# A post-norm attention and mixture-of-experts kernel: other places in the attention schedule, the tail of the last two batches moved, weight splits regrouped

## What is computed

```
qkv = x @ c_attn_w.T + c_attn_b                  # 16 heads of 16
q_lat, k_lat, v_lat = q@q2l.T+b, k@kv2l.T+b, v@kv2l.T+b     # 32 wide
q_lat, k_lat = rope(q_lat), rope(k_lat)
att = softmax(causal((q_lat @ wqk.T + b) @ k_lat.T * 32**-0.5))
x  = layernorm(x + (att @ v_lat @ l2o.T + b) @ cproj.T + b)
gates = top 2 of 8 of softmax(x @ gate_w)
y = sum over the two experts: w2 . gelu(ln(w1 . x + b1)) + b2, weighted
out = layernorm(x + ln(y + x))
```

## Time and profile before

| | us |
|---|---|
| median of 3 runs | 2278.8 |
| the three runs | 2265.12, 2283.3, 2278.8 |
| the profiled execution | 2262.56 |
| its span, first to last instruction | 2260.8 |
| granted TensorE clock, mean share of full speed | 0.949 |

### The profile page before, as it was taken

The page is one execution under the profiler, slowest core; times in us unless marked ns, Lnnn a source line. Parts: engine busy times, 40 slices in busy tenths (PEclk is TensorE's granted clock), DMA queues, the critical chain, the costliest instruction groups (busy, mean ns, idle before and its releaser), DMA issues. The chain is left out here.

```text
span 2260.8 us, 43557 instructions
## 1 busy us (share of the span) xinstructions
PE 2031.2 (90%) x12109; PEld 1414.5 (63%) x12109; DVE 1683.3 (74%) x4941; ACT 1403.8 (62%) x3324; POOL 1428.6 (63%) x1696
## 2 busy tenths in 40 slices
PE   4799999999999999999999999995399999999785
PEld 3555655655655655655565565543299999999664
DVE  3677677677777778768767777735588888888598
ACT  1266657656656665666665665664188888888565
POOL 2364565676665685477567566544677777777575
PEclk7799999999999999999999999986699999999998
DMA  6565556556645555555555564425022222222593
GB/s 180 137 139 149 123 121 170 123 117 149 152 106 131 152 129 136 154 122 125 145 124 120 139 157 106 106 56 212 20 73 76 74 75 74 77 74 74 192 313 131
DMA packets 165759, 284.56 MB, mean 126 GB/s; under 512 B 54000, under 2 KB 78216, under 8 KB 165384
## 3 DMA queue, kind: packets, MB, share of 16 engines
q1 hardware_dynamic: 146264, 244.87, 42.7%
q0 software_dynamic: 17152, 35.87, 5.2%
q10 hardware_dynamic: 2112, 1.05, 0.2%
HBM read 100.11 MB, written 38.22 MB: 61 GB/s over the span
## 5 line engine op out<-in xcount | busy, mean ns | idle before, releaser
L603 ACT ACTIVATE probs<-scores_T 128x512 f32<-128x512 f32 (+3 forms) x1536 | 660.0, 494 | 286.2 <-PE scores_T L474 269.9
L881 POOL TENSOR_SCALAR_AFFINE_SELECT probs<-probs 128x256 f32<-128x256 f32 x512 | 211.6, 421 | 506.8 <-ACT probs L603 505.0
L774 DVE TENSOR_REDUCE neg_part<-ring 128x1 f32<-128x512 f32 x512 | 333.5, 686 | 166.4 <-PE ring L533 164.4
L533 PE MATMUL ring<-k_stack,q_stack_b 96*128 96x512 f32 (+3 forms) x1024 | 401.1, 416 | 28.9 <-DVE neg_max L779 26.7
L474 PE MATMUL scores_T<-q_stack_b,k_stack 98*128 98x512 f32 (+3 forms) x1024 | 358.2, 394 | 14.2 <-ACT probs L603 12.9
L491 PE MATMUL o_ps<-probs,v_ones 128*17 128x512 f32 (+3 forms) x3072 | 334.9, 509 | 17.4 <-POOL probs L881 17.4
L779 DVE CUSTOM_DVE_ANT_0 ring<-ring,mask 128x384 f32<-128x384 f32 (+3 forms) x512 | 241.7, 510 | 94.5 <-PE ring L533 89.5
L533 PEld LDWEIGHTS ring<-k_stack,q_stack_b 96*128 96x128 f32 x1024 | 197.0, 194 | 169.0 <-DVE neg_max L779 67.2
L779 DVE CUSTOM_DVE_ANT_0 ring<-ring,mask,neg_part 128x384 f32<-128x384 f32 (+3 forms) x512 | 258.8, 554 | 34.8 <-PE ring L533 32.5
L474 PEld LDWEIGHTS scores_T<-q_stack_b,k_stack 98*128 98x128 f32 x1024 | 193.2, 195 | 127.2 <-ACT probs L603 100.4
L1216 ACT ACTIVATE o_sb<-ht_ps,ln_b,ln_g 128x128 f32<-128x128 f32 x544 | 217.1, 448 | 76.2 <-PE ht_ps L1165 73.2
(11 more groups left out here) (207 smaller groups left out, 4624.3 us busy)
## 6 DMA issues: line engine op xcount, KB each, us to landing
u_rot<-u SPq DMA_DIRECT2D x128, 256.0 KB
k_stack<-u_rot SPq DMA_DIRECT2D x128, 256.0 KB
lat_w<-lat_split SPq DMA_DIRECT2D x32, 512.0 KB
q_stack_a<-u_rot SPq DMA_DIRECT2D x64, 256.0 KB
q_stack_b<-u_rot SPq DMA_DIRECT2D x64, 256.0 KB
k_stack<-u SPq DMA_DIRECT2D x64, 256.0 KB
y<-y_rows SPq DMA_DIRECT2D x32, 512.0 KB, 6.0
x_raw<-in_xT SPq DMA_DIRECT2D x16, 512.0 KB, 5.8
```

Source lines behind the costliest of these rows:

```text
L533: nc.tensor.matmul(out[:, 0:k1 - k0], q_stack[qb // 4][0:3 * L, row_buf(n, qb // 4), h, P * (qb % 4):P * (qb % 4) + P], k_stack[0:3 * L, n ...
L603: nc.scalar.activation(probs[:, s % 2, h, cols], sc[t % 3][:, HALF - w:HALF], ACT.Exp).then_inc(exp_done, 1)
L774: nc.vector.tensor_reduce(neg_part[:, n % 2, part_col], src[:], AX_X, ALU.max, negate=True).then_inc(max_taken, 1)
L881: nc.gpsimd.affine_select(both, both, [[0, 2], [1, P]], ALU.is_ge, zero, base=0, channel_multiplier=-1).then_inc(kept, 1)
```

## The change

Three things, all of order:

1. `PLACES` and `LAGS` get other numbers. Sorted, SyncE's order of DMAs stays the same but for one item (STORE of batch 6 comes before PACK of unit 29). On GpSimd, in g0, the first k-rope instruction now stands before a SCAT, the first Y behind the first add of the rope (before it until now), and the second Y behind the second add; in g1 a SCAT that stood behind the k-rope's second instruction (the first sine) stands behind its fourth (the first add); ZB and NORM move a few places. On VectorE the second X pair moves behind two S, the second KL behind one or two S, and the C items come at half a slot apart and not a whole one. On TensorE C moves likewise, the second U of k and the first WQ move behind one to three other items, and the four V come without other items between them. On ScalarE NX, KH's second half and E move.
2. For batch 6, NX, ZT and G get a pace of 3 slots (4 before), and STORE, R, E, CNT and SCAT come 8.125 slots earlier, SCAT at a pace of 1. ZB of batch 7 gets a pace of 1. The items of `LAST_TAIL` no longer get the `LAGS`, so NORM of batch 7 comes behind the last mask of unit 31, and not before the last two.
3. In the second block ScalarE splits eight weights before NX of the second half (four before); VectorE does W 0 to 3 between the two routing groups and 4 to 14 at the end (0 to 12 at the end before); GpSimd does W 15 alone (13, 14 and 15 before).

```diff
--- before.py
+++ after.py
@@ -176,25 +176,26 @@
 
 
 PLACES = {
-    "B": (-6, 0.25), "LAT": (-54.625, 0.125), "Uq": (-50.125, 1), "SWAPq": (-50.75, 0.125), "ROPEq": (-44.25, 0),
-    "WQ": (-41.5, 1.875), "QL": (-40.75, 1.75), "STACKq": (-34.375, 0.125), "Uk": (-43.625, 0), "SWAPk": (-39, 0.5),
-    "ROPEk": (-37.75, 0.5), "KH": (-35.75, 2.25), "KL": (-33.375, 2.125), "STACKk": (-30, 5.75),
-    "S": (-27.75, 22.375), "MT": (-2.375, 0), "MD": (-3.375, 0), "PV": (5.5, 2), "OE": (11.5, 16.125),
-    "PACK": (23.75, 0.25), "RCP": (28.625, 0.125), "INV": (22.25, 0), "Y": (35.375, 1), "X": (-60.375, 3.75),
-    "V": (-22.25, 0.5), "RES": (17.5, 0.5), "ZB": (30.375, 3), "C": (39.625, 1), "NORM": (52.375, 0),
-    "NX": (51.875, 4), "ZT": (56.75, 4), "G": (60, 4), "STORE": (85.5, 0), "R": (88.875, 0.375),
-    "CNT": (94.375, 0.25), "SCAT": (102.625, 3.625), "SPREAD": (34.375, 0), "E": (94.25, 0)}
+    "B": (-13.125, 0.25), "LAT": (-54.125, 0), "Uq": (-50.375, 1), "SWAPq": (-50.625, 0.625), "ROPEq": (-44.25, 0),
+    "WQ": (-41, 1.5), "QL": (-40.375, 1.75), "STACKq": (-32.75, 0), "Uk": (-43.5, 0.5), "SWAPk": (-39.5, 0.5),
+    "ROPEk": (-38.5, 0.5), "KH": (-35.375, 2.75), "KL": (-33.625, 3.125), "STACKk": (-30.375, 4.875),
+    "S": (-27.75, 22.375), "MT": (-2.375, 1), "MD": (-4.625, 0.75), "PV": (5.5, 2), "OE": (11.375, 16.125),
+    "PACK": (28.625, 0.5), "RCP": (28.625, 0), "INV": (22.875, 0.5), "Y": (35.75, 1.5), "X": (-61, 5),
+    "V": (-21.625, 0), "RES": (16.5, 2.125), "ZB": (30.5, 3.625), "C": (40, 0.5), "NORM": (51.75, 0),
+    "NX": (47.5, 4.375), "ZT": (56.875, 4), "G": (60.25, 4), "STORE": (79.75, 0.5), "R": (88.875, 0.375),
+    "CNT": (94.625, 1), "SCAT": (102.125, 3.625), "SPREAD": (37, 1.25), "E": (91.5, 0.375)}
 
 LAST_TAIL = {
     "PACK": (12, 16), "SUM": (13.5, 0), "INVERT": (14, 0), "EXPAND": (15.5, 0), "COPY": (16, 0), "Y": (17.5, 0),
     "C": (22, 0.5), "NORM": (24.5, 0)}
-
-
-LAGS = {"sync": {"INV": 5.625, "X": 1.25, "LAT": 0.875, "RES": 1.625, "STORE": -0.125, "STACK": -0.125, "SPREAD": 0.75, "SWAP": 0.125},
+LAST_UNIT = ("PACK", "SUM", "INVERT", "EXPAND", "COPY", "Y")
+
+
+LAGS = {"sync": {"INV": 9, "X": 2.375, "LAT": 0.875, "RES": 2.75, "STORE": 3.75, "STACK": 1, "SPREAD": -3.125, "PACK": -1, "MD": 0.375},
         "tensor": {},
-        "scalar": {"KH": 1, "E": -0.5, "OE": -0.25, "ZT": 0.375, "U": -0.25, "B": -0.125},
-        "vector": {"X": 1, "RCP": 0.75, "KL": -0.375, "S": -0.125, "G": -0.25, "C": -0.125, "NX": -0.5, "R": 0.375, "MT": -0.5},
-        "gpsimd": {"ZB": 1.25, "NORM": -2.625, "Y": 0.125, "SCAT": 1.75, "B": 0.25}}
+        "scalar": {"KH": 0.875, "E": 6.25, "OE": -0.125, "ZT": -0.625, "U": -0.25, "B": -0.375, "WQ": -0.5, "V": 0.125, "MT": -0.75, "NX": -0.125},
+        "vector": {"X": 1.5, "RCP": 0.625, "KL": -0.375, "S": -0.125, "G": -0.25, "C": -0.125, "NX": 5.75, "R": 0.5, "MT": -0.5, "QL": -0.75},
+        "gpsimd": {"ZB": -1.25, "NORM": -5.375, "Y": -0.625, "SCAT": 2.25, "B": 0.25, "ROPE": -0.25}}
 
 
 def attention_phase(nc, dram, wts, consts, xs, lat_dram, inv_dram, x1_dram, token_of_row, routes, tail, attention,
@@ -285,8 +286,15 @@
 
             def put(name, *items):
                 first, pace = LAST_TAIL[name] if n == UNITS - 1 and name in LAST_TAIL else PLACES[name]
-                if name == "SCAT" and b == B - 2:
-                    pace = 0.9
+                if b == B - 2 and name in ("NX", "ZT", "G"):
+                    pace = 3
+                    first = PLACES["ZT"][0] + 2.25 if name == "G" else first
+                if b == B - 2 and name in ("STORE", "R", "E", "CNT", "SCAT"):
+                    (zt, _), (gate, slow) = PLACES["ZT"], PLACES["G"]
+                    first -= gate + slow * (TB - 1) - (zt + 2.25 + 3 * (TB - 1))
+                    pace = min(pace, 1)
+                if b == B - 1 and name == "ZB":
+                    pace = 1
                 at.extend((first + pace * i, it) for i, it in enumerate(items))
 
             put("LAT", ("LAT", n))
@@ -344,7 +352,8 @@
         def order_of(engine):
 
             lag = LAGS[engine]
-            return [it for _, it in sorted(placed, key=lambda p: p[0] + lag.get(p[1][0], 0))]
+            own = lambda it: (it[0] in LAST_TAIL and it[1] == (UNITS if it[0] in LAST_UNIT else B) - 1)
+            return [it for _, it in sorted(placed, key=lambda p: p[0] + (0 if own(p[1]) else lag.get(p[1][0], 0)))]
 
         main = {engine: order_of(engine) for engine in LAGS}
         of_tiles = lambda name, *tbs: [(name, B - 1, tb) for tb in tbs]
@@ -974,14 +983,14 @@
         table_loads = [(limit, "limit"), (slot_no, "slot_no"), (tile_row, "tile_row"),
                        (base0, "base"), (rows2, "rows2")]
         weights = lambda a, b: [("W", w) for w in range(a, b)]
-        hi_order = (13, 0, 14, 15, 1, 2, 3, 4, 5, 6, 7, 8, 9, 10, 11, 12)
+        hi_order = (15, 0, 1, 2, 3, 4, 5, 6, 7, 8, 9, 10, 11, 12, 13, 14)
         upper = lambda a, b: [("W", w) for w in hi_order[a:b]]
         route = lambda v: [("R", v, i) for i in range(R_STEPS)]
-        late_act = (of_tiles("NX", 0, 1, 2, 3) + of_tiles("ZT", 0, 1, 2, 3) + upper(0, 4) + of_tiles("NX", 4, 5, 6, 7)
-                    + [("E", B - 1)] + of_tiles("ZT", 4, 5, 6, 7) + upper(4, 7) + [("E", B)] + upper(7, len(parts)))
+        late_act = (of_tiles("NX", 0, 1, 2, 3) + of_tiles("ZT", 0, 1, 2, 3) + upper(0, 8) + of_tiles("NX", 4, 5, 6, 7)
+                    + [("E", B - 1)] + of_tiles("ZT", 4, 5, 6, 7) + upper(8, 11) + [("E", B)] + upper(11, len(parts)))
         late_dve = (of_last("INVERT") + of_last("COPY") + of_tiles("G", 0, 1, 2, 3) + of_tiles("C", 4, 5, 6, 7) + route(B - 1)
-                    + of_tiles("G", 4, 5, 6, 7) + route(B))
-        late_pool = (of_last("Y") + [("W", 13), ("NORM", B - 1, 1)] + weights(14, len(parts))
+                    + weights(0, 4) + of_tiles("G", 4, 5, 6, 7) + route(B))
+        late_pool = (of_last("Y") + [("W", 15), ("NORM", B - 1, 1)]
                      + [("SCAT", B - 1, k, tb) for k in range(2) for tb in range(TB // 2)]
                      + [("SCAT", B, k, tb) for k in range(2) for tb in range(TB // 2, TB)])
 
@@ -1054,15 +1063,15 @@
                 then(nc.vector.tensor_scalar(expert_f[:], expert_f[:], float(E - 1), None, ALU.min))
                 nc.vector.tensor_copy(routes["expert"][:], expert_f[0:1, :]).then_inc(done, 1)
                 nc.vector.tensor_copy(routes["ones2"][:], rows2[:]).then_inc(done, 1)
-                vector_items(dve, weights(0, 13))
-                dve.wait_ge(w_lo_ready, 13)
+                vector_items(dve, weights(4, 15))
+                dve.wait_ge(w_lo_ready, 15)
                 dve.wait_ge(done, 3)
 
             @block.gpsimd
             def _(pool):
                 nc.gpsimd.memset(experts["b2"][:].bitcast(F32), 0.0).then_inc(b_zeroed, 1)
                 gpsimd_items(pool, late_pool, None)
-                pool.wait_ge(w_lo2_ready, len(parts) - 13)
+                pool.wait_ge(w_lo2_ready, len(parts) - 15)
                 pool.wait_ge(scattered, 16 * 2 * TILES)
 
     return experts
```

## The result

The changed kernel takes 2220.1 us (median of 4 runs, 2216.8 to 2222.6) against 2276.8 for the kernel before (median of 4 runs, 2265.1 to 2283.3): a ratio of 0.9756, 95% interval 0.9719 to 0.9792, so 2.4% or 56 us faster. The forecast was 24 us, and the range ended at 2235. The profiled executions lie 40.1 us apart (spans 2260.8 and 2220.7): the one before was among the fastest of its kernel, which the forecast carried over as a constant.

| | before | after | |
|---|---|---|---|
| start to unit 0 | 106.4 | 105.5 | -0.9 |
| the eight g0 units | 371.9 | 359.4 | -12.4 |
| the eight g1 units | 378.4 | 369.5 | -8.8 |
| the eight g2 units | 322.9 | 322.9 | -0.1 |
| the seven g3 units | 313.1 | 304.1 | -9.0 |

What follows compares the result with a forecast made beforehand. Attention, two thirds of the span, was taken as TensorE's, losing to idle time and a falling clock. Terms 6 + 7 + 8 - 3 + 4.4 + 2 = 24 us took 2278.8 to 2255; range 2235 to 2280.

Steps and rivals of the forecast that it cites:

- KL in g0: VectorE's KL in g0 is held less by GpSimd: 1.2 us in five units, 6 us (0 to 8).
- X in g1: First X pair in g1 starts during a scatter and is stretched less: 1.4 us in five units, 7 us.
- rival A: In g1 a scatter makes the cast wait as an add does, and the clock falls as before: 2270, chance 0.18.
- The clock: TensorE's clock falls less in five g1 units after shorter idle: about half of 15 us, 8 us (0 to 15).
- New waits: Eight C at half a slot can push S back: 0.5 us per batch in six batches, 3 us lost.
- rival C: In g0 VectorE becomes the bound under eight C and TensorE stands at C: slower, 2304, chance 0.12.
- Unit 31: End of attention: two mask waits go, a new one costs 1.9 us, NORM ends the block: 4.4 us gained.
- Second block: Eleven weight splits follow the tables where thirteen did, so the last scatters come earlier: 2 us (0 to 4).
- seven behind it: In the second block seven scatters follow the one that stood through the splits; all come 1.9 us earlier.

Runs made afterwards that it cites:

- one_rope: Kernel before with only GpSimd's new order of k-rope, Y and scatter: ratio 0.9896 to the kernel before, 24 us faster.
- act_pool: Changed kernel with TensorE and VectorE sorted by the old tables, ScalarE and GpSimd by the new: ratio 0.9851 to the kernel before.
- xload3: Changed kernel with each batch's first x load issued by SyncE before PACK, some 9 us earlier: 2198.3 us, ratio 0.9678 to the kernel before.
- tail: Kernel before with only the tail of the last two batches moved and LAST_TAIL items without LAGS: ratio 0.9966, 8 us faster.
- one_c: Kernel before with only the C items at half a slot: ratio 1.0057, 13 us slower.
- late: Kernel before with only the weight splits of the second block regrouped: ratio 1.0005 to the kernel before.
- one_kl: Kernel before with only KH and KL moved: ratio 0.9967 to the kernel before.
- one_uk: Kernel before with only the second U of k moved: ratio 0.9983 to the kernel before.

## Why the prediction was wrong

The side was right and the size half of it, and that half is in part luck: two terms, X and the clock, 15 us in sum, did not come, and g3 and g1 gave 18 us that the sum did not have. By its own terms, against the profiled execution:

*KL in g0: 6 us, measured 12.4.* The mechanism held: Y behind the add, KL at 1.98 us. The term was too small twice. I took 1.2 of the 1.6 us that unit 24 showed, and the units lost 1.5 to 1.9; and I counted the five units with the long KL, while units 0, 4 and 24 lost 3.7 us more. Of the 12.4 us, 6.7 are idle time of TensorE and the rest its busy time, 1.7 of it the one fall of the clock in unit 4. `one_rope` shows the 12 us alone.

*X in g1: 7 us, measured a loss: the wait behind the pair went from 3.35 to 3.94 us, and in unit 5 from 1.23 to 3.12.* The step that failed is "The first pair keeps its place and its load. [...] So at 889.9 GpSimd is in the scatter." Only the load kept its place. GpSimd came 1.1 us earlier in the unit and VectorE 1.2 us, as TensorE's wait of 0.9 us ahead of WQ was gone and the unit's work moved up behind it (that chain is read from the order of events, no run cuts it). So the cast still began when the load landed, and then met the sine itself; in unit 5 it met nothing, and the wait for the load alone cost 3.12 us. Nor would the place have been enough. By the forecast's own rows the cast stood 0.5 us ahead of the sine (889.90, 890.40), and where it did begin 0.33 us ahead of it, in `act_pool`, 0.70 us into a scatter, it lost nevertheless:

```profile
1060.90 2.18 DVE L772 CAST x_hi<-x_raw 128x1024 fp32r<-128x1024 f32 x1 [0.64 <-DMA x_raw<-in_xT]
...
1060.20 1.01 POOL L948 DMA_INDIRECT token_of_row<-ids,slot  x1 [0.17 <-issue]
1061.23 1.29 POOL L886 TENSOR_TENSOR u_rot<-u_rot,sin 128x512 f32<-128x512 f32 x1
```

So rival A's outcome came in g1, by another cause. The KL of the earlier trace rows, on which the forecast leaned, kept its 0.69 us with a mask 0.64 us later, not a rope instruction queued right behind; the last section has the counts. The rule of the Trainium skill weighed in the prediction (SBUF — State Buffer, "SBUF: two separate sides"), that who starts first holds the pair, gave 13 us for this part. The full change gave none of it. In `xload3`, units 9, 17, 21 and 25, the traces agree with it: VectorE starts and GpSimd is stretched. In the 16 cases of the last section they don't: there VectorE's instruction has the earlier start in the record, and ends behind GpSimd's.

*The clock: 8 us, measured none.* In the five g1 units that it was for (9, 13, 17, 21, 25) low clock stayed at 37.5 us in sum; the wait that comes before it had not shrunk. Over all the units it went from 51 to 48 us, 1.7 us of time: units 4 and 15 lost their falls, unit 1 half of its, and unit 5 got a new one. The estimate was fair for the case that didn't come: `xload3`, with the wait gone, has 23 us less of it in the units, 12 us of time.

*New waits: 3 us lost.* As a term on its own it was too low: C alone cost 13 us. Beside the shorter KL it cost nothing, and undoing it was no gain. I had priced C against the kernel before; its price hung on the other edit, as rival C ("where KL leaves a backlog") said without the sum using it.

*What the sum didn't have: g3, 9 us, and g1, 8.8 us without X.* The prediction looked at the long waits. The g3 units had waits of 0.3 to 0.7 us, mostly, among them one for the copy into `k_stack`; 5.4 us of idle time went there, the rest is one fall of the clock (1.7 us) and busy time. Of g1's 8.8 us only 1.6 are idle time: the 0.9 us ahead of WQ went and 0.6 came back at X. The rest is busy time of TensorE, though g1 had 3.4 us more of the lower clock; three matmuls of each unit moved over into g2, which grew no longer. Why TensorE's own time for the same matmuls fell by 15 us over the span stays open: at most some 4 us of it go with 8.5 us less at the lower clock over the span (an estimate), the rest lies between the row maxima and their neighbours, and no run isolated it.

*Unit 31: 4.4 us, measured 3.3 up to the start of the second block, which is how the forecast counted (4.7 up to the last PV, as in the table); `tail` 8 us.* Right in its steps: a new mask wait (1.13 us, charged 1.9), none of the old, the end with NORM. The sum has some luck in it. I had not seen the 1.6 us more at the unit's start, nor the clock: the unit had 27.5 us at the lower level before and 30.7 after. Less half of that, an estimate, it went from 34.6 to 28.3 us up to the last PV, and to 28.7 in `tail`.

*Second block: 2 us, measured 6.1 from its own start (4.7 in the table, which counts from the last PV).* 2.3 less in splits is right; the last splits began 44.3 us into the block for 44.4, where I had 0.4 later. I kept "seven behind it"; it became four, 3 x 1.27 = 3.8 us more, as eleven scatters were out when the last splits began, and eight before. 2.3 and 3.8 are the 6.1.

The rest, from 40 us in the profile to 56 in the medians, is for 14 us the profiled execution of before, 2262.6 us to its kernel's 2276.8, and for 2.5 the one after, the slowest of its four. The one before had a granted clock of 0.949; of the 22 runs of that kernel beside `one_c` 19 had less. How much low clock a profile shows varies: with nearly the same steady order, `late` and `one_kl` have 69 and 68 us in the units, `tail` 51 and `one_uk` 46, to its 51. And the parts don't add: GpSimd's order is 24 us alone and 42 in the whole, and one edit is a loss alone and none beside it.

## What to carry to other kernels

When an edit takes away a wait upstream, every engine below it shifts in time, and what collided is to be placed anew against what did not shift, here a load that is used some 11.5 us after its issue. Price an edit in the kernel as the other edits leave it, and ask of the cheapest order edit first whether an operand can be there earlier: one load issued sooner gave some 20 us on top. A chain that runs in every unit pays in many small waits at once, and their sum is a term of its own.

## What the runs showed of the hardware

Whether VectorE's cast or subtraction from SBUF to SBUF suffers when it begins during a scatter of GpSimd hangs, in these traces, on what is queued behind the scatter and how soon. In the traces of all these kernels, 44 casts, subtractions and KLs began during a scatter with a 128x512 rope instruction directly behind it. In the 28 in which that instruction began 0.84 us or more later, they took their least (0.69, 1.23), and it was the rope instruction that was stretched, or nothing. In the 16 in which it began within 0.71 us they ended only behind it, at 1.9 to 2.6 us, even two KLs that would have been over at 0.69 with the add at 0.67 and at 0.71 (2.51 and 2.56 us). With a mask (128x256) behind the scatter instead, the 64 KLs that began 0.26 to 0.94 us ahead of it took 0.66 to 0.69 us, and only the 11 that began within 0.11 us of it lost (1.07 to 1.76 us; `one_rope` and `rope_uk`). So the claim of the queued instruction seems to be there before its recorded start, longer for the rope than for a mask; that reading fits all of these, but wasn't tested by itself.

A wait of TensorE of 3.1 to 3.9 us was followed by very different times at 1.2 GHz: units 13 and 17 of the changed kernel have waits of 3.8 and 3.9 us with nearly the same work around them, and 3.4 and 13.7 us at the lower level; they take 46.6 and 50.7 us. After waits of 1.2 to 2.2 us there was anything from none (unit 5 of the kernel before) to 10.2 us (unit 13 of `xload3`). One such difference is worth as much as some of the edits here, so the edits had to be read from units and not from single times.
